# Masks of the attention scores written into PSUM by ScalarE and VectorE instead of by products with the identity

## The chip, the cores and the metric

The kernel runs on one core of one Trainium2 chip. The metric is the device time of one execution in microseconds. Engines are named as in the profile: PE is TensorE's matrix product, PEld its weight load, DVE is VectorE, ACT is ScalarE, POOL is GpSimd, SP is SyncE, which starts the transfers here.

## The reference, cut to what matters

One layer with two branches over x of shape 8 x 1024 x 256: after a layer norm, an attention branch and a branch of eight gated experts; their outputs and x are added. The experts' part is not touched. The attention:

```
xn = layernorm(x)
q, k, v = split(xn @ w_qkv + b_qkv), 16 heads of 16
scores = q @ k.T * 16 ** -0.5
4 global heads: scores masked where i - j < 0
12 local heads: scores masked where i - j < 0 or i - j > 64
ctx = softmax(scores) @ v
x = x + ctx @ w_out + b_out + experts(xn)
```

## The kernel before, in words

**Chunks.** The work goes in 16 chunks of 512 tokens (two for each of the 8 sequences; even chunks are the first half, odd ones the second). A planner (class `Plan` and the functions `add_...` and `..._groups`) writes down one list of stages, in one order, for all chunks. Every engine's program walks this one list and issues what is its own in each stage, so the order of each engine's queue is the order of the list. Semaphores join the engines. `weave(main, side)` mixes two lists of groups evenly.

**PSUM banks** are handed out by turns: each stage names the banks it uses (`uses`), and before a product writes into a bank, `take` waits until the reader of the bank's previous turn has counted up `bank_read[i]`.

**The attention is done in two passes.** The first finds for each query and head the maximum of the scores (*peaks*), the second computes the scores again with the maximum subtracted inside the product, as additional rows of the operands.
- *Local peaks*, stage `lpeak(t, grp)`, 12 a chunk: a product with the identity matrix lays the mask in a bank (L726, 512 columns), then eight products of 64 rows by 128 columns add the scores (L732). VectorE reduces the bank (L1197).
- *Global peaks*, stage `gpeak(t, j)`, 10 in an even chunk and 26 in an odd one: four products (L746), ahead of them a mask by the identity (L743) on the diagonal blocks only, 4 a chunk. VectorE reduces (L1204).
- Both use banks 5, 6 and 7 in turn. Counting them 0, 1, 2, ... over the two kinds, stage n can start when the reduction of stage n - 3 is done. Local peaks are stages 0 to 11. Diagonals are stages 12, 14, 17, 21 in an even chunk and 16, 22, 29, 37 in an odd one.
- *Local scores*, stage `lscore(grp, half, pair)`, 12 a chunk: mask by the identity (L766), eight products (L772), then ScalarE's exponential out of the bank (L1021). Banks 6 and 5 in turn, so score m can start when the exponential of m - 2 is done. The weighted sums of the values are L793, their transposes L837 (`cout`).
- *Global scores* follow (L807, L825) and are not masked by products.

**What is woven around them.** The peak stages of a chunk are woven, two at a time, into its experts (`x`, `c`: products of 512 columns, L587; `product`: the gates spread over a bank (L701), two VectorE products (L1273, L1276), ScalarE's PH copy (L1003); `mix`, L714; `open`, L675). ScalarE's copy `prod` out of `x` is L993. The stage `rows` turns the found maxima (L757), ScalarE copies them out of bank 4 (L1015) and a transfer brings them to the operands. The layer norm of the next chunk (`norm`, nine pieces on VectorE) is spread over the peak stages too. The local scores are woven with the next chunk's `turn` (transposes L605, ScalarE's XH copy L928, VectorE's subtraction XL L1145 and scan L1152) and `parts` (products L587, ScalarE L934, and three VectorE steps L1168, L1171, L1173). The order there, for one chunk (k is the score's number): scores 0, 1; turn 0; scores 2, 3; mix; values; turn 1; scores 4, 5; values; rows; scores 6, 7; parts(1,0); values, cout; parts(1,1); scores 8, 9; values; parts(0,0); scores 10, 11; parts(0,1); values, cout, values. The last chunk has no next one, and what is left of its experts is woven in instead.

Of the kernel before, what the change touches and what calls it, by code (L numbers as in the profile page):

```python
# [9 lines left out]
ACT = mybir.ActivationFunctionType  # L10
AX_X = mybir.AxisListType.X

P = 128
# [28 lines left out]
class Plan:  # L42
# [6 lines left out]
    def add(self, kind, *key, uses=()):  # L49
        self.stages.append((kind, *key))  # L50
        self.count[kind] = self.count.get(kind, 0) + 1
        self.place[(kind, *key)] = self.count[kind]
        for what in uses:
            self.turn[what] = self.turn.get(what, 0) + 1
            self.slot[(kind, *key), what] = self.turn[what]

# [9 lines left out]
def mixer_layer(  # L66
# [68 lines left out]

    def add_lpeak(ch, t, grp):
        add_on("lpeak", ch, t, grp, uses=[peak_use()])

    def add_gpeak(ch, t, j):
        add_on("gpeak", ch, t, j, uses=[peak_use()])  # L140

# [27 lines left out]

    def add_lscore(ch, grp, half, pair):  # L170
        add_on("lscore", ch, grp, half, pair, uses=[score_use(), exp_use()])

# [82 lines left out]
    def peak_groups(ch):  # L255
        c = ch % NC
        order = [[(add_lpeak, ch, t, grp)] for t in range(T) for grp in range(NL // 4)]
        order[-1].append((add, "found", ch, 0))
        gpeaks = [[(add_gpeak, ch, t, j)] for t in range(T) for j in range(c * T + t + 1)]
# [118 lines left out]
    with ctx:  # L378
# [136 lines left out]
        dve_step, pool_step, blank, cleared, selected, readied = (sem(n) for n in ("dve_step", "pool_step", "blank", "cleared", "selected", "readied"))  # L515
        global_masked = sem("global_masked")
        columns_ps, biases_in, split_hi, split_lo, turned_w, fold_ps = (sem(n) for n in ("columns_ps", "biases_in", "split_hi", "split_lo", "turned_w", "fold_ps"))
# [27 lines left out]
        def out_of_bank(*stage):  # L545

            i = bank_of(*stage)
            return bank_read[i], use(f"bank{i}", *stage)

        def on_diagonal(ch, j, half):  # L550
# [30 lines left out]
        def tensor_program(e):  # L581
# [12 lines left out]
            for stage in plan.stages:  # L594
# [124 lines left out]
                elif kind == "lpeak":  # L719
                    ch, t, grp = key  # L720
                    i, = where[stage]
                    which = 1 if ch % NC == 0 and t == 0 else 0
# [3 lines left out]
                    e.matmul(psum(i).rearrange("p (a k) -> p a k", a=4), ident_b[:, :],  # L726
                             peak_mask_l[:, which, :].unsqueeze(1).to_broadcast([P, 4, P]), start=True, stop=False, skip_group_check=True)
                    for a in range(4):
# [7 lines left out]
                elif kind == "gpeak":  # L736
# [3 lines left out]
                    q.wait_ge(global_in, 128 * (ch + 1))  # L740
                    take(i, *stage)
                    if diag:
                        e.matmul(psum(i).rearrange("p (a k) -> p a k", a=4), ident_b[:, :], peak_mask_g[:, :].unsqueeze(1).to_broadcast([P, 4, P]),  # L743
                                 start=True, stop=False, skip_group_check=True)
                    for g in range(NG):
# [14 lines left out]
                elif kind == "lscore":  # L760
# [3 lines left out]
                    q.wait_ge(ones_set, 2)  # L764
                    take(i, *stage)
                    e.matmul(psum(i).rearrange("p (w q) -> p w q", w=8), ident_b[:, :],  # L766
                             mask_l[:, :].unsqueeze(1).to_broadcast([P, 8, WINDOW]), start=True, stop=False, skip_group_check=True)
                    for a in range(2):
# [147 lines left out]
        def scalar_program(e):  # L916
            q = Seq(e)

            for stage in plan.stages:
# [75 lines left out]
                elif kind == "product":  # L995
# [7 lines left out]
                    e.activation(PH[:, h, :], prod[:, j % 3, :], ACT.Copy).then_inc(phi)  # L1003

                elif kind == "rows":
                    ch, which = key
# [90 lines left out]
        def vector_program(e):  # L1097
            q = Seq(e, dve_step)

            for stage in plan.stages:  # L1100
# [99 lines left out]
                elif kind == "gpeak":  # L1200
                    ch, t, j = key
                    i, = where[stage]
                    q.wait_ge(gpeaks_ps, nth(*stage))
                    e.tensor_reduce(block_peak[ch % NC][:, t, :, j], psum(i).rearrange("p (a k) -> p a k", a=4), AX_X, ALU.max).then_inc(bank_read[i])  # L1204

                elif kind == "found":
# [392 lines left out]
```

## Time and profile before

| | |
|---|---|
| median of 3 runs | 1655.23 us (1655.19 to 1657.1) |
| the profiled execution | 1654.62 us, span 1652.9 us |
| granted TensorE clock | 0.996 of full speed |
| TensorE busy (products) | 1563.5 us, 95% |
| VectorE busy | 937.7 us, 57% |
| ScalarE busy | 684.4 us, 41% |
| GpSimd busy | 284.2 us, 17% |

Busy times are unions of the instructions' spans on one engine. Consecutive products overlap in the trace, so the mean duration of one is longer than its place in the stream; the chain of waits gives the place.

### The profile page before, as it was taken

What the parts mean: (1) busy time and instruction counts of PE and PEld (TensorE: products, weight loads), DVE (VectorE), ACT (ScalarE), POOL (GpSimd) and SP (SyncE); (2) the same over time, 40 slices, a digit from 0 to 9 for tenths busy, and PEclk for the clock granted to TensorE, in tenths of its full rate; (3) what the DMA queues carried; (4) which work ended last, traced back from release to release, by engine and by line L of the source; (5) the groups of instructions that cost most, each with busy time, mean ns of one, the idle gap of its engine ahead of it and who ended that gap; (6) DMA issues with size and microseconds to landing.
All of it is one profiled execution on the core that took longest, in us unless ns stands there. A gap on an engine that the chain in (4) does not pass through costs nothing.

```text
span 1652.9 us, 36914 instructions
## 1 busy us (share of the span) xinstructions
PE 1563.5 (95%) x15489; PEld 1112.8 (67%) x15489; DVE 937.7 (57%) x2048; ACT 684.4 (41%) x1224; POOL 284.2 (17%) x346
## 2 busy tenths in 40 slices
PE   5899999999999999999999999999999999999997
PEld 4576675767757676676757767576675767667674
DVE  6665672737537484564837567274763748447461
ACT  3426245261543517243362523626254351634425
POOL 2011121211112111121201212021111201112111
PEclk9999999999999999999999999999999999999999
DMA  8514417072350906218071350806326080530800
GB/s 207 63 31 88 80 34 123 10 117 51 76 89 4 151 15 104 61 38 130 4 122 45 77 91 21 125 21 106 62 64 100 4 139 27 96 69 23 132 4 14
DMA packets 128186, 116.48 MB, mean 70 GB/s; under 512 B 19251, under 2 KB 127668, under 8 KB 127972
## 3 DMA queue, kind: packets, MB, share of 16 engines
q1 hardware_dynamic: 128020, 114.12, 38.5%
q8 instruction: 122, 2.00, 0.6%
q14 instruction: 44, 0.36, 0.1%
HBM read 73.43 MB, written 34.34 MB: 65 GB/s over the span
## 4 chain that ended last, share of the span: by engine, by line
PE 76%; DVE 14%; ACT 5%; issue 4%; POOL 1%; DMA 0%; DVEq 0%; ACTq 0%; POOLq 0%
PE PS L587 33%; PE PS L714 8%; DVE block_peak L1204 4%; PE PS L793 3%; PE PS L825 3%; PE PS L732 3%; PE PS L856 3%; PE PS L766 3%; PE PS L807 3%; PE PS L772 3%; DVE prod L1273 2%; PE PS L726 2%; DVE prod L1276 2%; ACT HE L1029 2%; PE PS L746 2%
## 5 line engine op out<-in xcount | busy, mean ns | idle before, releaser
L1446 POOL TENSOR_TENSOR PL<-prod,PH 128x512 fp32r<-128x512 f32 x128 | 164.5, 1285 | 792.7 <-ACT PH L1003 792.7
L1003 ACT ACTIVATE PH<-prod 128x512 fp32r<-128x512 f32 x128 | 80.8, 631 | 428.8 <-DVE prod L1276 428.8
L587 PE MATMUL PS<-XH,WH 128*128 128x512 f32 x512 | 220.4, 430 | 4.5 <-DVE XL L1145 1.9
L587 PE MATMUL PS<-XH,WL 128*128 128x512 f32 x512 | 203.6, 398 | 0.0
L587 PE MATMUL PS<-XL,WH 128*128 128x512 f32 x512 | 203.2, 397 | 0.0
L1204 DVE TENSOR_REDUCE block_peak<-PS 128x4 f32<-128x512 f32 x288 | 186.9, 684 | 4.2 <-PE PS L746 4.2
L993 ACT ACTIVATE prod<-PS 128x512 f32<-128x512 f32 x128 | 76.3, 596 | 231.3 <-PE PS L587 220.3
L1029 ACT ACTIVATE HE<-PS 128x512 f32<-128x512 f32 (+1 forms) x320 | 159.7, 552 | 26.1 <-PE PS L807 23.5
L1197 DVE TENSOR_REDUCE peak<-PS 128x4 f32<-128x512 f32 x192 | 125.6, 685 | 41.0 <-PE PS L732 41.0
L1273 DVE TENSOR_TENSOR prod<-PS,prod 128x512 f32<-128x512 f32 x128 | 88.1, 689 | 104.6 <-PE PS L701 104.6
L714 PE MATMUL PS<-UH,PH 128*128 128x256 f32 x512 | 139.5, 306 | 0.0
L1439 POOL TENSOR_SCALAR_AFFINE_SELECT HE<-HE 128x256 f32<-128x256 f32 x128 | 50.7, 409 | 478.9 <-ACT HE L1029 476.4
L1286 DVE RECIPROCAL cinv<-PS 128x16 f32<-128x16 f32 x64 | 16.3, 254 | 205.2 <-PE PS L837 205.2
L714 PE MATMUL PS<-UL,PH 128*128 128x256 f32 x512 | 126.0, 280 | 0.0
L587 PE MATMUL PS<-CH,WH 128*128 128x512 f32 x256 | 109.2, 427 | 9.1 <-DVE prod L1276 9.0
L587 PEld LDWEIGHTS PS<-XH,WH 128*128 128x128 f32 x512 | 96.9, 189 | 26.6 <-DVE WL L1341 2.2
L1021 ACT ACTIVATE HE<-PS 128x512 f32<-128x512 f32 x192 | 104.6, 596 | 21.5 <-PE PS L772 21.5
L587 PEld LDWEIGHTS PS<-XH,WL 128*128 128x128 f32 x512 | 96.7, 189 | 23.1
L807 PE MATMUL PS<-area 99*128 99x256 bf16 (+1 forms) x640 | 100.4, 267 | 7.8 <-ACT HE L1029 3.9
L587 PEld LDWEIGHTS PS<-XL,WH 128*128 128x128 f32 x512 | 97.3, 190 | 14.6
L746 PE MATMUL PS<-area 96*128 96x128 bf16 x1152 | 100.8, 220 | 5.8 <-DVE block_peak L1204 4.9
L807 PEld LDWEIGHTS PS<-area 99*128 99x128 bf16 x640 | 41.8, 98 | 93.5 <-ACT HE L1029 56.9
(195 smaller groups left out, 3154.8 us busy)
## 6 DMA issues: line engine op xcount, KB each, us to landing
parts_d<-area SPq DMA_DIRECT2D x32, 768.0 KB, 5.1
area<-parts_d SPq DMA_DIRECT2D x128, 192.0 KB, 12.4
area<-parts_d SPq DMA_DIRECT2D x32, 576.0 KB, 12.5
tok<-in_L_attn_x_dram SPq DMA_DIRECT2D x16, 512.0 KB, 6.5
xt<-in_L_attn_x_dram SPq DMA_DIRECT2D x16, 512.0 KB, 3.9
out_dram<-xt SPq DMA_DIRECT2D x16, 512.0 KB, 3.7
area<-parts_d SPq DMA_DIRECT2D x96, 64.0 KB, 5.9
Vs<-Va SPq DMA_DIRECT2D x24, 204.0 KB, 7.6
```

The source lines that it names most:

```text
L587: ins = e.matmul(ps, a, b, start=first and k == 0, stop=last and k == n - 1, skip_group_check=True)
L714: ins = e.matmul(out_half(t), (PH, PL)[part][:, h, t * P:(t + 1) * P], u[:, j, :], start=False, stop=False, skip_group_check=True)
L746: ins = e.matmul(psum(i, lo=P * g, hi=P * (g + 1)), QS[0:G16, g, t * P:(t + 1) * P], KG[0:G16, g, j * P:(j + 1) * P], start=(g == 0 and no ...
L807: ins = e.matmul(psum(i, lo=HALF * a + lo, hi=HALF * (a + 1)), KG[0:KSTK, g, j * P:(j + 1) * P], QS[0:KSTK, g, half * HALF + lo:(half + 1) ...
L993: e.activation(prod[:, j % 3, :], psum(2), ACT.Copy).then_inc(bank_read[2])
L1003: e.activation(PH[:, h, :], prod[:, j % 3, :], ACT.Copy).then_inc(phi)
L1021: e.activation(HE[:, k, :], psum(i), ACT.Exp, scale=SCALE).then_inc(bank_read[i])
L1029: e.activation(two(HE[:, k, :], lo), two(psum(i), lo), ACT.Exp, scale=SCALE).then_inc(bank_read[i])
L1197: e.tensor_reduce(peak[:, t, NG + 4 * grp:NG + 4 * (grp + 1)], psum(i).rearrange("p (a k) -> p a k", a=4), AX_X, ALU.max).then_inc(bank_re ...
L1204: e.tensor_reduce(block_peak[ch % NC][:, t, :, j], psum(i).rearrange("p (a k) -> p a k", a=4), AX_X, ALU.max).then_inc(bank_read[i])
L1273: e.tensor_tensor(prod[:, r, :], psum(4), prod[:, r, :], ALU.mult).then_inc(bank_read[4])
L1446: e.tensor_tensor(PL[:, j % 2, :], prod[:, j % 3, :], PH[:, j % 2, :].bitcast(F32), ALU.subtract).then_inc(plo)
```

## The change

The masks of most stages are no longer laid by a product. A new stage kind, `seed`, writes the mask into the bank ahead of the stage it belongs to: ScalarE does it for the peaks (an activation Copy of the broadcast bf16 mask into PSUM), VectorE for the local scores (a copy). The scores' products then add onto it. A seed stands in the list two stages ahead of its own stage: right behind peak n - 2 for peak n, right behind score m - 2 for score m. It waits until the bank's previous reader is done. Stages 0, 1 and 2 of the peaks and scores 0 and 1 of each chunk keep their identity product; peaks off the diagonal have no mask, as before. For this the banks of the peaks and scores are named when the groups are made, and the seed claims the bank in place of its stage (`claim`).

```diff
+    def add_scores(stage, uses):
+        bank, *slots = uses
+        laid = stage in where
+        if laid:
+            add(*stage, uses=slots)
+        else:
+            add(*stage, uses=uses)
+            where[stage] = [int(bank[-1])]
+        where[stage] += [int(u[-1]) for u in slots]
+
+    def add_seed(bank, *stage):
+        add("seed", *stage)
+        plan.claim(stage, [bank])
+        where[stage] = [int(bank[-1])]
...
     def local_groups(ch):
         units = [(grp, half) for grp in range(1, 1 + NL // 4) for half in range(2)]
+        scores = [(ch, grp, half, pair, score_use()) for grp, half in units for pair in range(2)]
         order = []
         for n, (grp, half) in enumerate(units):
-            order.append([(add_lscore, ch, grp, half, pair) for pair in range(2)])
+            order.append([])
+            for m in (2 * n, 2 * n + 1):
+                order[-1].append((add_lscore, *scores[m]))
+                if m + 2 < len(scores):
+                    order[-1].append((add_seed, scores[m + 2][4], "lscore", *scores[m + 2][:4]))
...
     def peak_groups(ch):
-        order = [[(add_lpeak, ch, t, grp)] for t in range(T) for grp in range(NL // 4)]
+        order = [[(add_lpeak, ch, t, grp, peak_use())] for t in range(T) for grp in range(NL // 4)]
+        gpeaks = [[(add_gpeak, ch, t, j, peak_use())] for t in range(T) for j in range(c * T + t + 1)]
+        for n, ((stage, *key),) in enumerate(order + gpeaks):
+            if stage is add_lpeak and n > 2:
+                order[n - 2].append((add_seed, key[-1], "lpeak", *key[:-1]))
+            elif stage is add_gpeak and key[2] == c * T + key[1]:
+                (order + gpeaks)[n - 2].append((add_seed, key[-1], "gpeak", *key[:-1]))
...
(TensorE, lpeak; lscore likewise with local_seeded, gpeak's diagonals likewise)
-                    take(i, *stage)
-                    e.matmul(psum(i)..., ident_b[:, :], peak_mask_l..., start=True, stop=False)
+                    if stage in laid:
+                        q.wait_ge(seeded, peaks_laid.index(stage) + 1)
+                    else:
+                        take(i, *stage)
+                        e.matmul(psum(i)..., ident_b[:, :], local_peak_mask(ch, t), start=True, stop=False)
...
(ScalarE)
+                elif kind == "seed":
+                    of, i = key, bank_of(*key)
+                    take = bank_read[i], use(f"bank{i}", *of) - 1
+                    if of[0] == "lpeak":
+                        q.wait_ge(*take)
+                        e.activation(psum(i)..., local_peak_mask(*of[1:3]), ACT.Copy).then_inc(seeded)
+                    elif of[0] == "gpeak":
+                        q.wait_ge(*take)
+                        e.activation(psum(i)..., peak_mask_g[:, :]..., ACT.Copy).then_inc(seeded)
...
(VectorE)
+                elif kind == "seed" and key[0] == "lscore":
+                    i = bank_of(*key)
+                    q.wait_ge(bank_read[i], use(f"bank{i}", *key) - 1)
+                    e.tensor_copy(psum(i)..., mask_l[:, :]...).then_inc(local_seeded)
```

## Rows read from the trace of the kernel before

**Rows 1.** The page: busy time by engine, and shares of the last chain.

```profile
PE 1563.5 (95%) x15489; PEld 1112.8 (67%) x15489; DVE 937.7 (57%) x2048; ACT 684.4 (41%) x1224; POOL 284.2 (17%) x346
...
PE 76%; DVE 14%; ACT 5%; issue 4%; POOL 1%; DMA 0%; DVEq 0%; ACTq 0%; POOLq 0%
```

**Rows 2.** Sums by stage: start:end length, then busy (instructions) of PE, PEld, DVE, ACT, POOL.

```profile
480.40:523.10 42.70, 41.32 (x325) 30.59 (x324) 32.03 (x71) 8.64 (x14) 9.64 (x8) 1.00 0.09 28
523.10:541.90 18.80, 18.80 (x354) 14.41 (x356) 11.82 (x21) 11.30 (x21) 4.44 (x5) 1.00 0.14 45
571.10:618.80 47.70, 46.04 (x388) 33.88 (x386) 39.90 (x85) 8.35 (x14) 9.00 (x7) 1.00 0.16 36
618.80:638.00 19.20, 19.02 (x357) 14.49 (x356) 12.81 (x25) 11.65 (x22) 5.06 (x5) 1.00 0.14 44
...
588.50:618.80 30.30, 29.29 (x229) 23.07 (x226) 27.57 (x66) 5.86 (x10) 5.75 (x5) 1.00 0.01 4
```

**Rows 3.** Groups by line, TensorE: count, busy us, mean ns, idle us before.

```profile
L726 PE MATMUL PS<-peak_mask_l,ident_b 128*128 128x512 bf16 x192 | 74.3, 387 | 0.6 <-DVE peak L1197 0.6
L766 PE MATMUL PS<-mask_l,ident_b 128*128 128x512 bf16 x192 | 74.1, 386 | 8.8 <-DVE block_peak L1204 8.8
```

**Rows 4.** The chain of waits, peaks 4 and 5 of chunk 5: start, us, what.

```profile
576.79 0.22 PE PS L726
...
577.35 0.32 PE PS L726
577.67 0.34 PE PS L732 x8
```

**Rows 5.** Groups by line, VectorE and ScalarE, each operation of 512 elements.

```profile
L1171 DVE CAST area<-rest 128x512 bf16<-128x512 f32 x64 | 27.4, 427 | 2.2
L1320 DVE MEMSET PS<- 128x512 f32 x2 | 1.0, 485 | 0.2
L1145 DVE TENSOR_TENSOR XL<-PS,XH 128x512 fp32r<-128x512 f32 x32 | 22.1, 692 | 33.7 <-ACT XH L928 33.6
L993 ACT ACTIVATE prod<-PS 128x512 f32<-128x512 f32 x128 | 76.3, 596 | 231.3 <-PE PS L587 220.3 <-POOL PL L1446 11.0
L1003 ACT ACTIVATE PH<-prod 128x512 fp32r<-128x512 f32 x128 | 80.8, 631 | 428.8 <-DVE prod L1276 428.8
```

**Rows 6.** ScalarE in order of time, peak stage of chunk 5: start, us.

```profile
576.57 0.63 ACT L1003 ACTIVATE PH<-prod 128x512 fp32r<-128x512 f32 x1 [2.84 <-DVE prod L1276]
...
601.47 0.63 ACT L1003 ACTIVATE PH<-prod 128x512 fp32r<-128x512 f32 x1 [2.56 <-DVE prod L1276]
```

**Rows 7.** TensorE in order of time, peak stage of chunk 5.

```profile
601.89 0.61 PE L746 MATMUL PS<-area 96*128 96x128 bf16 x8
```

**Rows 8.** The chain of waits, local stage of chunk 4.

```profile
525.53 1.50 PE PS L714 x12
...
529.09 0.57 PE PS L793 x32
...
529.87 0.32 PE PS L766
...
530.88 1.48 PE PS L587 x6
...
534.91 0.23 PE PS L766
...
538.92 1.48 PE PS L587 x6
```

**Rows 9.** VectorE in order of time, local stage of chunk 4.

```profile
524.24 0.18 DVE L1225 TENSOR_TENSOR peak_t_global<-peak_rest,peak_t_global 128x16 bf16<-128x16 f32 x1
...
529.46 1.27 DVE L1152 TENSOR_TENSOR_SCAN rest<-PS,carry,XH 128x512 f32<-128x512 f32 x1
...
536.92 0.69 DVE L1173 TENSOR_TENSOR area<-rest,area 128x512 bf16<-128x512 f32 x1
```

**Rows 10.** ScalarE in order of time, local stage of chunk 4.

```profile
523.74 1.08 ACT L1021 ACTIVATE HE<-PS 128x512 f32<-128x512 f32 x2 [1.33 <-PE PS L772]
```

More of the change, by code:

```diff
@@ L52, in add, with claim @@
         self.place[(kind, *key)] = self.count[kind]
+        self.claim((kind, *key), uses)
+    def claim(self, stage, uses):
         for what in uses:
             self.turn[what] = self.turn.get(what, 0) + 1
-            self.slot[(kind, *key), what] = self.turn[what]
+            self.slot[stage, what] = self.turn[what]
     def nth(self, kind, *key):
@@ L134, in mixer_layer, with add_lpeak, add_gpeak @@
     NORM = ("moments", "start", "square", "correct", "square", "correct", "square", "correct", "scale")
[L136 to L140, printed above, removed]
+    def add_lpeak(ch, t, grp, bank):
+        add_scores(("lpeak", ch, t, grp), [bank])
+    def add_gpeak(ch, t, j, bank):
+        add_scores(("gpeak", ch, t, j), [bank])
+    def add_scores(stage, uses):
[11 more added lines that the diff above has]
+        where[stage] = [int(bank[-1])]
     def add_turn(ch, k):
@@ L168, in add_mix, with add_lscore @@
         add("mix", ch, j, part, uses=[f"phl{j % 2}"] if part else [])
-    def add_lscore(ch, grp, half, pair):
-        add_on("lscore", ch, grp, half, pair, uses=[score_use(), exp_use()])
+    def add_lscore(ch, grp, half, pair, bank):
+        add_scores(("lscore", ch, grp, half, pair), [bank, exp_use()])
     def add_lav(ch, grp, half):
@@ L256, in peak_groups @@
         c = ch % NC
-        order = [[(add_lpeak, ch, t, grp)] for t in range(T) for grp in range(NL // 4)]
+        order = [[(add_lpeak, ch, t, grp, peak_use())] for t in range(T) for grp in range(NL // 4)]
[5 more added lines that the diff above has]
+                (order + gpeaks)[n - 2].append((add_seed, key[-1], "gpeak", *key[:-1]))
         order[-1].append((add, "found", ch, 0))
-        gpeaks = [[(add_gpeak, ch, t, j)] for t in range(T) for j in range(c * T + t + 1)]
         gpeaks[2].append((add_rows, ch, 0))
@@ L515, in mixer_layer @@
         dve_step, pool_step, blank, cleared, selected, readied = (sem(n) for n in ("dve_step", "pool_step", "blank", "cleared", "selected", "readied"))
-        global_masked = sem("global_masked")
+        global_masked, seeded, local_seeded = (sem(n) for n in ("global_masked", "seeded", "local_seeded"))
         columns_ps, biases_in, split_hi, split_lo, turned_w, fold_ps = (sem(n) for n in ("columns_ps", "biases_in", "split_hi", "split_lo", "turned_w", "fold_ps"))
@@ L548, in out_of_bank, with local_peak_mask @@
             return bank_read[i], use(f"bank{i}", *stage)
+        laid = [stage[1:] for stage in plan.stages if stage[0] == "seed"]
+        local_laid = [of for of in laid if of[0] == "lscore"]
+        peaks_laid = [of for of in laid if of[0] != "lscore"]
+        def local_peak_mask(ch, t):
+            return peak_mask_l[:, 1 if ch % NC == 0 and t == 0 else 0, :].unsqueeze(1).to_broadcast([P, 4, P])
         def on_diagonal(ch, j, half):
@@ L721, in tensor_program @@
                     i, = where[stage]
-                    which = 1 if ch % NC == 0 and t == 0 else 0
                     q.wait_ge(local_in, 128 * (ch + 1))
                     q.wait_ge(kept, ch + 1)
-                    take(i, *stage)
-                    e.matmul(psum(i).rearrange("p (a k) -> p a k", a=4), ident_b[:, :],
-                             peak_mask_l[:, which, :].unsqueeze(1).to_broadcast([P, 4, P]), start=True, stop=False, skip_group_check=True)
+                    if stage in laid:
+                        q.wait_ge(seeded, peaks_laid.index(stage) + 1)
+                    else:
+                        take(i, *stage)
+                        e.matmul(psum(i).rearrange("p (a k) -> p a k", a=4), ident_b[:, :], local_peak_mask(ch, t),
+                                 start=True, stop=False, skip_group_check=True)
                     for a in range(4):
@@ L740, in tensor_program @@
                     q.wait_ge(global_in, 128 * (ch + 1))
-                    take(i, *stage)
                     if diag:
-                        e.matmul(psum(i).rearrange("p (a k) -> p a k", a=4), ident_b[:, :], peak_mask_g[:, :].unsqueeze(1).to_broadcast([P, 4, P]),
-                                 start=True, stop=False, skip_group_check=True)
+                        q.wait_ge(seeded, peaks_laid.index(stage) + 1)
+                    else:
+                        take(i, *stage)
                     for g in range(NG):
@@ L764, in tensor_program @@
                     q.wait_ge(ones_set, 2)
-                    take(i, *stage)
-                    e.matmul(psum(i).rearrange("p (w q) -> p w q", w=8), ident_b[:, :],
-                             mask_l[:, :].unsqueeze(1).to_broadcast([P, 8, WINDOW]), start=True, stop=False, skip_group_check=True)
+                    if stage in laid:
+                        q.wait_ge(local_seeded, local_laid.index(stage) + 1)
+                    else:
+                        take(i, *stage)
+                        e.matmul(psum(i).rearrange("p (w q) -> p w q", w=8), ident_b[:, :],
+                                 mask_l[:, :].unsqueeze(1).to_broadcast([P, 8, WINDOW]), start=True, stop=False, skip_group_check=True)
                     for a in range(2):
@@ L1003, in scalar_program @@
                     e.activation(PH[:, h, :], prod[:, j % 3, :], ACT.Copy).then_inc(phi)
+                elif kind == "seed":
[3 more added lines that the diff above has]
+                        q.wait_ge(*take)
+                        e.activation(psum(i).rearrange("p (a k) -> p a k", a=4), local_peak_mask(*of[1:3]), ACT.Copy).then_inc(seeded)
+                    elif of[0] == "gpeak":
+                        q.wait_ge(*take)
+                        e.activation(psum(i).rearrange("p (a k) -> p a k", a=4), peak_mask_g[:, :].unsqueeze(1).to_broadcast([P, 4, P]),
+                                     ACT.Copy).then_inc(seeded)
                 elif kind == "rows":
@@ L1204, in vector_program @@
                     e.tensor_reduce(block_peak[ch % NC][:, t, :, j], psum(i).rearrange("p (a k) -> p a k", a=4), AX_X, ALU.max).then_inc(bank_read[i])
+                elif kind == "seed" and key[0] == "lscore":
+                    i = bank_of(*key)
+                    q.wait_ge(bank_read[i], use(f"bank{i}", *key) - 1)
+                    e.tensor_copy(psum(i).rearrange("p (w q) -> p w q", w=8),
+                                  mask_l[:, :].unsqueeze(1).to_broadcast([P, 8, WINDOW])).then_inc(local_seeded)
                 elif kind == "found":
```

## The prediction

> **What bounds the kernel now.** I read the page first, then the sums by stage, then the chain of waits, then single engines where the change lands. The page shows TensorE busy 95% of the span and on 76% of the chain that ended last [rows 1]: its instructions in order are the time, save where they wait. A pass over one chunk has three stages, and the windows show what stands beside TensorE in two of them [rows 2]. The peak stage of an even chunk takes 42.7 us with VectorE busy for 32.0; that of an odd chunk takes 47.7 with VectorE busy for 39.9, so the odd one is nearly bound by two engines. The local stage takes about 19 us with TensorE never idle (18.80 of 18.80) and VectorE busy for 11.8 to 12.8. The global stage isn't touched. So a TensorE instruction that goes is worth its place in the stream, if what replaces it is in time; the seeds that replace it sit in the fixed order of two other engines' queues, and that is where I look.
>
> **What goes.** Of the mask products, 144 of 192 on L726 (9 of 12 a chunk), 160 of 192 on L766 (10 of 12) and all 64 on L743 (4 a chunk, as the code has it) go [rows 3]. Their mean of about 386 ns is no price, since ends overlap. The chain gives the place they hold: 0.22 us for the first of a pair of peak products and 0.32 for the second, where the half-width products behind it start late; their eight products hold 0.34 [rows 4]. Per chunk that is 4 x 0.22 + 5 x 0.32 = 2.48 us for the local peaks (stage 3 is the second of its pair, then four pairs), 4 x 0.22 = 0.88 for the diagonals, and 10 x 0.22 = 2.2 for the local scores (0.32 once). Over 16 chunks: about 90 us, if nothing came late.
>
> **The price of a seed.** No row shows either operation: 512 bf16 read with a broadcast pattern, written to PSUM as f32. For ScalarE the nearest are 596 ns from PSUM and 631 from SBUF [rows 5]; I take 0.6 and see no reason for it to leave 0.55 to 0.65. For VectorE the bounds are far apart: the CAST of 512 elements within SBUF took 427 ns, a memset of 512 in PSUM 485, and the subtraction of 512 that reads PSUM 692 [rows 5]. I take 0.69: the only 512-element copy below it touches no PSUM, and the memset reads nothing.
> The Trainium skill speaks to this choice: "VectorE: DVE Perf Modes", section "Why PSUM operands drop a tier", says that the fast mode of a single-source operation with 32-bit data needs its tensors in SBUF and that with PSUM it runs at one element a cycle. By that rule 0.69 stands; by the CAST's row alone the sum below would come out at the price of the first rival. The trace has nothing that decides between them.
>
> **Peak stage, even chunks.** ScalarE has 8.6 us of work in 42.7 [rows 2], so 13 seeds x 0.6 = 7.8 us fit. A seed waits for the reduction three peaks earlier and for ScalarE's queue ahead of it. In most pairs 3 us or more of TensorE's other work lie between, and the seed is done in time. The exception is the pair of stages 4 and 5: their seeds are queued behind the PH copy of product 1. I put that wait at 0.3 us. VectorE has gaps enough in this stage, and its own work does not grow. Gain: 2.48 + 0.88 - 0.3 = 3.05, say 3.0 us a chunk, 24 us for eight.
>
> **Peak stage, odd chunks.** The pairs come closer. Pair 4, 5 follows pair 2, 3 with only four small products (L675) between. The PH copy of product 1 holds ScalarE from 576.57 to 577.20 [rows 6]; seed 4 follows to 577.8, seed 5 to 578.3, so that pair ends near 578.7 instead of 578.02 [rows 4]: +0.7 us, with stage 3's 0.32 already counted. The next three pairs have a transform or a mix ahead of each; they give 3 x 0.54 back, less 0.1, which makes -0.8 by the end of the local peaks. From there VectorE leads: 26 reductions of some 0.6 us, the normalization of the next chunk and the products leave it 2.7 us without work in the last 30.3 of the stage [rows 2], and what TensorE has gained is waited away. In this stretch two seeds are late. In stage 14's group the seed is queued ahead of ScalarE's `rows` copy, which frees bank 4 for product 3; that eats most of what is left, since product 3's VectorE step was due anyway. And stage 22's diagonal is seeded behind the PH copy of product 4, which ends at 602.10 [rows 6]: seeded at 602.7, while its products started at 601.89 before [rows 7]. That is +0.8, and product 5 follows it. Stage 29 repeats this with about 0.4, mostly absorbed by VectorE. I take +0.9 a chunk, seven chunks: 6.3 us lost. Bounds: -1.5 (to win: most of those 2.7 us, at no cost of waits) and +2. The last chunk is woven otherwise (no next chunk): -0.7.
>
> **Local stage.** Here VectorE gets 10 seeds, 6.9 us on top of 12, and they stand in its order among the next chunk's work. I follow the chain of chunk 4 [rows 8] with VectorE's rows [rows 9]; k is the number of the score stage, 0 to 11.
> - Seeds 2 and 3: VectorE is busy until 524.42 with the global peaks' parts [rows 9], and the exponentials of 0 and 1 end at 524.8 [rows 10]. Seeds end at 525.14 and 525.75; scores 3 end at 526.05 instead of 525.53. Two mask products are gone and the stage is still 0.5 late.
> - Seeds 4 and 5 follow VectorE's first turn (subtraction and scan); they end at 528.9, and scores 5 end at 529.18 instead of 529.09 [rows 8].
> - Seeds 6 and 7 are queued behind the second turn. Its scan ran from 529.46 to 530.73 [rows 9], and scores 6 began at 529.87 [rows 8], before the scan's end, which cost nothing. Now scores 6 must wait for it: the scan, 0.5 later with its turn, ends at 531.26, the seeds at 532.0 and 532.6, scores 7 at 532.9 instead of 530.88 [rows 8]: 2.0 late.
> - Scores 8 and 9 are free of this and win 0.45.
> - Seeds 10 and 11 are queued behind the three VectorE steps of parts(1,1). These ended 2.70 after the transform (534.91 to 537.61) [rows 8, 9]. The transform now ends at 536.94, so the steps at 539.64, the seeds at 540.37 and 540.98, scores 11 at 541.27 instead of 538.92 [rows 8].
> So the local stage becomes 2.35 us longer, 2.2 us of removed products included. With seeds at 0.43 the same walk ends at +1.0. Fifteen chunks: +35.2 us (15 at 0.43). The last chunk has no turns and parts in this stage and wins 1.3. Behind the stage nothing changes: VectorE has room there and the loads of the next stacks have tens of us until use.
>
> **The sum.** -24.0 + 6.3 - 0.7 + 35.2 - 1.3 = +15.5 us. The profiled execution took 1654.6 (span 1652.9), 0.6 below the median of 1655.2. 1654.6 + 15.5 = 1670.1, by the median 1670.7: 0.9% slower. What a measurement of this kernel can tell from no change is about 0.2%, 3.3 us, so the border runs at 1658.5.
>
> **Rivals.**
> 1. VectorE lays a mask in 0.43 us. The mechanism is the same, but each of the two exposed queues (turn 1, parts(1,1)) carries two seeds of 0.43: 1670.7 - 15 x 1.35 = 1650.5, faster. For it: the CAST's row. Against it: the VectorE row that has a source and a PSUM side took 692 [rows 5]. It decides from about 0.49 us a seed, where the local stage's loss (1.3) equals what the peak stages win. 13%.
> 2. The odd peak stages keep what their local peaks win (-1.0 instead of +0.9), because VectorE catches up in gaps that I count as closed: 1657.4, no change that could be told. For it: VectorE's 7.8 idle us in that stage. Against it: the order behind PH. 10%.
> 3. Nothing waits and the whole 90 us come off: 1565. For it: 95% TensorE. Against it: scores 6 began before the end of a scan that their seeds must follow. 4%.
> 4. The ScalarE seeds, waiting for reductions, hold up its transform copies and with them VectorE's products in every peak stage; the even chunks then win only 1.0 each: 1670.7 + 16 = 1687. For it: one queue for waits of two kinds. Against it: some 2 us of room before each copy in the even chunks. 12%.
> My forecast has the remaining 61%, with a range of its own of 1662 to 1680.
>
> **How the numbers follow.** Faster: rival 3, two thirds of rival 1, a little of rival 2: 0.15. Same: the rest of rival 1 and half of rival 2: 0.10. Slower: 0.75. The range from 1650 to 1684 leaves out rival 3, the far side of rival 1 and half of rival 4.
>
> **What the profile after will show.** Right: TensorE waits on L772 for VectorE's seed, in the third and the sixth pair of each local stage, 1.5 to 2 us and about 1; the local stage near 21.3 us, even peak stages near 39.7, odd ones near 48.5; a seed at 0.69 us on VectorE and 0.6 on ScalarE. In odd chunks the products of stages 4 and 22 wait for ScalarE. Wrong: a VectorE seed under 0.5 us, or local stages no longer than before.

## The result and the profile after

The changed kernel takes 1699.7 us (median of 4 runs, 1697.2 to 1702.4) against 1655.2 (4 runs, 1653.0 to 1657.1): the ratio is 1.0271, interval 1.0259 to 1.0283, so 2.7% slower. The forecast was 1670.7, and its range ended at 1684. The profiled execution took 1702.4 us with a span of 1700.7, 47.8 more than before, and its granted clock is 0.976 where it was 0.996.

The page of the changed kernel: busy time by engine, and the chain's shares, to be laid beside [rows 1].

```profile
PE 1515.6 (89%) x15121; PEld 1104.4 (65%) x15121; DVE 1033.3 (61%) x2208; ACT 805.4 (47%) x1432; POOL 282.7 (17%) x346
...
PE 66%; DVE 19%; ACT 8%; issue 5%; POOL 1%; DMA 0%; DVEq 0%; ACTq 0%; POOLq 0%
```

TensorE is busy for 48 us less in a span that is 48 us longer: it stands still for 96 us more. On the chain VectorE and ScalarE have gained 8 of the 10 points that TensorE lost. Who makes it stand still is in the sums by pair of the waits (the product that waits, the instruction that ends the wait, then total us, how often, the longest):

```profile
PE PS L817 <- DVE PS L1265: 60.2, 90, 2.1
PE PS L741 <- ACT peak_f L1071: 12.7, 7, 1.8
PE PS L774 <- ACT PS L1055: 12.6, 9, 1.6
PE PS L788 <- ACT PS L1058: 10.4, 14, 0.8
```

L817 is the local scores' product and L1265 VectorE's seed for it; L774 and L788 are the peaks' products, L1055 and L1058 ScalarE's seeds; L741 is `product`, L1071 ScalarE's `rows` copy. The seeds themselves, in the groups by line:

```profile
L1265 DVE CAST PS<-mask_l 128x512 f32<-128x512 bf16 x160 | 102.3, 684 | 14.1 <-ACT HE L1077 14.0
L1055 ACT ACTIVATE PS<-peak_mask_l 128x512 f32<-128x512 bf16 x144 | 82.7, 592 | 21.1 <-DVE peak L1253 21.0
L1058 ACT ACTIVATE PS<-peak_mask_g 128x512 f32<-128x512 bf16 x64 | 38.1, 595 | 31.3 <-DVE block_peak L1260 31.2
```

684 ns and 592 to 595: the prices taken were 0.69 and 0.6. Now the span, cut at the first mask product of each peak stage, at that of each local stage and at the last product of L838, and summed over the chunks of both traces:

| stages | before | after | difference | forecast |
|---|---|---|---|---|
| setup, to the first peak | 85.6 | 87.5 | +1.9 | 0 |
| 8 even peak stages | 342.5 | 314.5 | -28.0 | -24.0 |
| 7 odd peak stages | 334.2 | 346.4 | +12.3 | +6.3 |
| 15 local stages | 288.0 | 349.5 | +61.5 | +35.2 |
| 15 global stages | 507.0 | 507.6 | +0.7 | 0 |
| last chunk | 95.7 | 95.1 | -0.6 | -2.0 |

Together they make the 47.8 us; differences are taken before rounding. (The setup is of no account: its work isn't touched, and over all the kernels below its length lay anywhere between 84.2 and 87.5.) The local stages hold the loss and most of the miss. Their windows, first chunk 4's, then chunk 6's (columns as [rows 2], then granted clock, DMA share, GB/s):

```profile
534.32:555.80 21.48, 17.77 (x347) 13.66 (x347) 17.90 (x32) 11.85 (x21) 4.41 (x5) 1.00 0.12 40
737.16:760.15 22.99, 19.28 (x347) 14.65 (x347) 17.97 (x32) 11.85 (x21) 4.43 (x5) 0.93 0.11 37
```

Both hold the same 347 products, the same work on the other engines, and TensorE stands still for the same 3.71 us. Yet chunk 6 is 1.51 us longer, all of it in TensorE's busy time, and its granted clock is 0.93. Cut finer, four microseconds each at the same places of the two stages, chunk 4 first:

```profile
540.16:544.16 4.00, 1.87 (x64) 1.52 (x61) 3.06 (x4) 2.89 (x6) 2.00 (x3) 1.00 0.02 5
544.16:548.16 4.00, 4.00 (x52) 2.89 (x52) 2.90 (x5) 1.35 (x3) 0.41 (x1) 1.00 0.03 7
...
743.00:747.00 4.00, 1.87 (x64) 1.52 (x61) 3.06 (x4) 2.89 (x6) 2.00 (x3) 1.00 0.03 7
747.00:751.00 4.00, 4.00 (x45) 2.80 (x43) 1.83 (x3) 1.36 (x3) 0.41 (x1) 0.57 0.01 3
```

The first window of each holds the wait for score 6, with TensorE busy for 1.87 us of 4. They are alike to the last digit but for the transfers. Behind it chunk 4 goes on at full clock, while chunk 6 runs the next stretch at half of it, 1.2 GHz instead of 2.4, and gets 45 products done where chunk 4 got 52. Such a stretch at half clock is called a fall below; it counts for the stage in which it begins. The trace's record of the granted clock has 4 before, one in the setup and three in the last chunk, and 23 after: 13 of the 19 new ones in local stages and 6 in odd peak stages. In the odd peak stages the same pair can be set side by side, chunk 3 without and chunk 5 with a fall:

```profile
383.06:431.29 48.23, 42.50 (x375) 32.58 (x373) 40.01 (x85) 15.34 (x27) 8.93 (x7) 1.00 0.14 34
...
494.81:534.32 39.51, 37.75 (x312) 29.29 (x311) 31.94 (x71) 15.58 (x27) 9.60 (x8) 1.00 0.10 30
...
584.78:634.51 49.73, 43.99 (x375) 33.74 (x374) 40.02 (x85) 15.34 (x27) 8.94 (x7) 0.97 0.16 35
634.51:658.48 23.97, 19.41 (x349) 14.84 (x347) 19.07 (x36) 12.40 (x22) 5.03 (x5) 0.93 0.11 36
```

Idle 5.73 and 5.74, length 1.50 apart. So a fall costs 1.5 us, and 19 of them make 28.5 us. They were counted in the profiled execution: 1702.4 - 28.5 = 1673.9, 3.8 above the 1670.1 that was forecast for it. That they come so close is in part luck: without falls the stages miss by -4.0 (even peaks), -3.0 (odd peaks), +6.8 (local) and +4.0 (the rest), which nearly cancel. The second line is the even peak stage of chunk 4, 3.2 us shorter than in [rows 2]; the fourth is chunk 5's local stage, with a fall.

The waits themselves stand in order of time. TensorE in the local stage of chunk 4, products of the scores:

```profile
536.35 0.41 PE L817 MATMUL PS<-area 99*128 99x64 bf16 x8 [0.49 <-DVE PS L1265]
536.94 0.41 PE L817 MATMUL PS<-area 99*128 99x64 bf16 x8 [0.19 <-DVE PS L1265]
539.83 0.63 PE L817 MATMUL PS<-area 99*128 99x64 bf16 x16
543.19 0.41 PE L817 MATMUL PS<-area 99*128 99x64 bf16 x8 [1.95 <-DVE PS L1265]
543.77 0.41 PE L817 MATMUL PS<-area 99*128 99x64 bf16 x8 [0.18 <-DVE PS L1265]
548.07 0.64 PE L817 MATMUL PS<-area 99*128 99x64 bf16 x16
551.58 0.41 PE L817 MATMUL PS<-area 99*128 99x64 bf16 x8 [0.71 <-DVE PS L1265]
552.17 0.41 PE L817 MATMUL PS<-area 99*128 99x64 bf16 x8 [0.19 <-DVE PS L1265]
```

These are scores 2, 3, then 4 and 5 together, 6, 7, 8 and 9 together, 10, 11. VectorE in the same stretch:

```profile
535.59 1.29 DVE L1265 CAST PS<-mask_l 128x512 f32<-128x512 bf16 x2
...
541.26 1.27 DVE L1208 TENSOR_TENSOR_SCAN rest<-PS,carry,XH 128x512 f32<-128x512 f32 x1
542.46 1.26 DVE L1265 CAST PS<-mask_l 128x512 f32<-128x512 bf16 x2
...
550.23 0.69 DVE L1229 TENSOR_TENSOR area<-rest,area 128x512 bf16<-128x512 f32 x1
550.84 1.28 DVE L1265 CAST PS<-mask_l 128x512 f32<-128x512 bf16 x2
```

Seeds 6 and 7 start when the scan of the second turn is done, 10 and 11 behind the last step of parts(1,1): the two places that the forecast named. ScalarE in the peak stage of chunk 5:

```profile
590.27 0.63 ACT L1048 ACTIVATE PH<-prod 128x512 fp32r<-128x512 f32 x1 [2.28 <-DVE prod L1338]
590.81 1.62 ACT L1055 ACTIVATE PS<-peak_mask_l 128x512 f32<-128x512 bf16 x3
```

The PH copy waits for VectorE's product for 2.28 us, and the seeds of peak 4 and its followers wait behind it; peak 4 starts 1.40 us late.

### The profile page after: what moved, and what is told of

It reads as the page before. It is cut to its first block, busy times and chain, and to the rows that moved or that the text cites. A ratio compares the mean times of both kernels' runs of the same rounds, so it can differ in the third digit from the quotient of the medians.

```text
span 1700.7 us, 36626 instructions
## 1 busy us (share of the span) xinstructions
PE 1515.6 (89%) x15121; PEld 1104.4 (65%) x15121; DVE 1033.3 (61%) x2208; ACT 805.4 (47%) x1432; POOL 282.7 (17%) x346
## 3 DMA queue, kind: packets, MB, share of 16 engines
q8 instruction: 119, 1.95, 0.5%
## 4 chain that ended last, share of the span: by engine, by line
PE 66%; DVE 19%; ACT 8%; issue 5%; POOL 1%; DMA 0%; DVEq 0%; ACTq 0%; POOLq 0%
PE PS L627 33%; PE PS L754 8%; DVE PS L1265 3%; PE PS L788 3%; PE PS L870 3%; PE PS L901 3%; DVE prod L1335 3%; DVE prod L1338 3%; ACT HE L1085 2%; PE PS L852 2%; PE PS L838 2%; PE PS L882 2%; PE PS L774 2%; PE PS L956 2%; DVE block_peak L1260 2%
## 5 line engine op out<-in xcount | busy, mean ns | idle before, releaser
L627 PE MATMUL PS<-XH,WH 128*128 128x512 f32 x512 | 225.9, 441 | 4.4 <-DVE XL L1201 1.9
L627 PE MATMUL PS<-XH,WL 128*128 128x512 f32 x512 | 208.2, 407 | 0.0
L627 PE MATMUL PS<-XL,WH 128*128 128x512 f32 x512 | 207.8, 406 | 0.0
L754 PE MATMUL PS<-UH,PH 128*128 128x256 f32 x512 | 144.5, 314 | 0.0
L1077 ACT ACTIVATE HE<-PS 128x512 f32<-128x512 f32 x192 | 109.8, 597 | 52.9 <-PE PS L817 52.7
L754 PE MATMUL PS<-UL,PH 128*128 128x256 f32 x512 | 131.0, 288 | 0.0
L817 PE MATMUL PS<-area 99*128 99x64 bf16 x1536 | 73.9, 196 | 60.3 <-DVE PS L1265 60.2
L817 PEld LDWEIGHTS PS<-area 99*128 99x128 bf16 x1536 | 58.8, 99 | 87.5 <-DVE PS L1265 78.7
L1265 DVE CAST PS<-mask_l 128x512 f32<-128x512 bf16 x160 | 102.3, 684 | 14.1 <-ACT HE L1077 14.0
## 6 DMA issues: line engine op xcount, KB each, us to landing
area<-parts_d SPq DMA_DIRECT2D x32, 576.0 KB, 12.3
```

The lines of the kernel that those rows point to most:

```text
L627: ins = e.matmul(ps, a, b, start=first and k == 0, stop=last and k == n - 1, skip_group_check=True)
L754: ins = e.matmul(out_half(t), (PH, PL)[part][:, h, t * P:(t + 1) * P], u[:, j, :], start=False, stop=False, skip_group_check=True)
L817: ins = e.matmul(psum(i, lo=(4 * a + w) * WINDOW, hi=(4 * a + w + 1) * WINDOW), KL[0:KSTK, l, k0:k0 + P], QS[0:KSTK, NG + l, k0:k0 + WINDO ...
L1077: e.activation(HE[:, k, :], psum(i), ACT.Exp, scale=SCALE).then_inc(bank_read[i])
L1265: e.tensor_copy(psum(i).rearrange("p (w q) -> p w q", w=8), mask_l[:, :].unsqueeze(1).to_broadcast([P, 8, WINDOW])).then_inc(local_seeded)
```

## The experiments

All were timed beside the kernel before, which measured 1654.1 in the first set (e1 to e4), 1656.0 in the second (e5, e6, e7, e9) and 1654.9 with e10. The theory: the local scores' seeds come late in VectorE's queue, their waits cost what they are long, and the granted clock falls behind them and costs the rest. Rivals: the peaks' seeds cause it; the missing instructions or busier engines, not the waits, bring the clock down; VectorE has too much to do as such. One table for all, idle being TensorE's time without a product in the local stages of chunks 4 and 5 and in the peak stage of chunk 5. Idle and falls are those of the one profiled execution, which needn't be the median one:

| kernel | median, ratio (interval) | idle, us | falls in local, odd peak stages |
|---|---|---|---|
| before | 1655.2 | 0.0, 0.2, 1.7 | 0, 0 |
| changed | 1699.7, 1.0271 (1.0259 to 1.0283) | 3.7, 4.6, 5.7 | 13, 6 |
| e1 | 1638.9, 0.992 (0.9895 to 0.9946) | 0.0, 0.4, 5.7 | 0, 10 |
| e2 | 1711.5, 1.0344 (1.0327 to 1.0361) | 3.7, 4.3, 1.6 | 9, 0 |
| e3 | 1684.8, 1.0184 (1.0168 to 1.0199) | 0.8, 1.8, 5.6 | 0, 9 |
| e4 | 1609.5, 0.9729 (0.9714 to 0.9743) | 0.0, 0.2, 2.5 | 0, 0 |
| e5 | 1668.4, 1.0069 (1.0045 to 1.0094) | 2.0, 2.9, 5.7 | 2, 10 |
| e6 | 1632.4, 0.9862 (0.9847 to 0.9876) | 0.0, 0.4, 5.0 | 0, 5 |
| e7 | 1633.6, 0.9869 (0.9854 to 0.9884) | 0.0, 0.4, 5.4 | 0, 2 |
| e9 | 1617.8, 0.9783 (0.9765 to 0.9802) | 1.4, 1.6, 2.4 | 0, 0 |
| e10 | 1600.0, 0.9666 (0.965 to 0.9682) | 0.1, 0.3, 2.4 | 0, 0 |

**e1, the peaks' seeds alone.**

```diff
-                if m + 2 < len(scores):
+                if m + 2 < len(scores) and False:
```

> The changed kernel with the masks of all local scores laid by TensorE again; the 13 ScalarE seeds a chunk for the peaks stay. Theory (queue waits, and a granted clock that falls after them): local stages back to 18.8 us at clock 1.000; even peak stages 3.5 us shorter than before, as in the changed kernel's trace (39.2 for 42.7), so 8 x -3.5 = -28; odd peak stages between +0.5 (clock 1.000, as in chunk 3 of the changed kernel) and +1.9 a chunk: 1655 - 28 + 3 to 14 = 1630 to 1641, faster than before. Rival (writing PSUM from other engines slows TensorE's own products everywhere): slower than 1655. Rival (the loss sits in the odd peak stages alone): near 1690.

The median is 15 us below that of the kernel before. The local stage of chunk 4 and the peak stage of chunk 5:

```profile
517.12:536.14 19.02, 19.02 (x357) 14.54 (x357) 12.02 (x22) 11.29 (x21) 4.45 (x5) 1.00 0.14 46
...
565.11:616.24 51.13, 45.41 (x376) 35.44 (x374) 40.16 (x85) 15.35 (x27) 8.94 (x7) 0.93 0.16 34
```

The local stage is back at 19.0, and the 15 together take 289.6 us: all but 1.5 of their 61.5 us come from the scores' seeds. The peak stage stands still for 5.7 us as in the changed kernel, but here the clock fell twice in it; over the seven odd ones it fell ten times. The five executions differ by as much: 1636.8 us at a mean clock of 0.992, 1648.4 at 0.984. The trace is of the last of these, the slowest, so ten falls are more than the median execution had.

**e2, the scores' seeds alone.**

```diff
-            if stage is add_lpeak and n > 2:
+            if stage is add_lpeak and False:
...
-            elif stage is add_gpeak and key[2] == c * T + key[1]:
+            elif stage is add_gpeak and key[2] == c * T + key[1] and False:
```

> The changed kernel with all masks of the peaks laid by TensorE again; only VectorE's 10 seeds a chunk for local scores 2 to 11 stay. Theory: peak stages as before (42.7 and 47.7), local stages 22.5 (even) and 23.7 (odd) where the clock falls, 21.0 and 22.2 where it does not: 1655 + 15 x 2.8 + 0 to 15 falls x 1.5 us = 1697 to 1720. If the waits of odd peak stages were needed for the fall of the clock in local stages, the low end. Rival (the peaks' seeds carry the loss): under 1665.

57 us slower; less e1's 15 that makes 42 of the 44.5. Peak stages are as before. Local stages without and with a fall (chunks 7 and 4):

```profile
841.77:864.25 22.48, 17.96 (x349) 13.73 (x347) 18.84 (x36) 12.21 (x22) 5.03 (x5) 1.00 0.11 38
...
536.48:559.45 22.97, 19.26 (x347) 14.71 (x347) 17.96 (x32) 11.87 (x21) 4.43 (x5) 0.93 0.11 37
```

**e3, zero products in the waits.** Nothing is left out; ahead of the waits of scores 2, 6 and 10 TensorE adds products with a tile of zeros onto a bank, 13 a chunk.

```diff
+                        for _ in range({2: 2, 6: 8, 10: 3}.get(4 * (grp - 1) + 2 * half + pair, 0) if ch + 1 < CHUNKS else 0):
+                            e.matmul(psum(0)..., ident_b[:, :], zeros_b[:, :]..., start=False, stop=False)
```

> The changed kernel with products of zeros added onto bank 0 ahead of the waits of local scores 2 (two), 6 (eight) and 10 (three), 512 columns each, in all chunks but the last: TensorE does more, but stands still for less; the seeds come as late as before. Theory (half of the local stages' loss is the granted clock, which falls to 1.2 GHz because TensorE stood still): local stages at clock 1.000, 21.0 even and 22.2 odd, 13 falls x 1.5 us gone: about 1680 against 1700. Rival (the clock falls for another reason, and waits alone are the loss): 1700 or, with 2.8 us of products a chunk that don't fit, up to 1715.

This separates the length of a wait from the fall behind it. The local stages of chunks 4 and 5:

```profile
528.98:550.47 21.49, 20.71 (x360) 14.76 (x360) 17.91 (x32) 11.87 (x21) 4.43 (x5) 1.00 0.12 40
...
628.95:651.64 22.69, 20.88 (x362) 14.82 (x360) 19.05 (x36) 12.42 (x22) 5.02 (x5) 1.00 0.11 38
```

Chunk 4's stage is as long as in the changed kernel (21.49, 21.48), with 13 more products in it. The local falls are gone, 13 to 0, and the local stages together went from 349.5 to 330.7 us. The whole is 14.9 us faster though TensorE does more. VectorE is as busy as before, so its load doesn't bring the clock down; TensorE standing still does. (The zero products also make up for the missing mask products; that these don't matter is seen in e5 and e10.) The odd peak stages, not filled, went on falling.

**e4, only the seeds that come in time.** The peaks' seeds without stages 4 and 5 and without diagonals in odd chunks, of the scores' seeds only 8 and 9, none in the last chunk.

```diff
-                if m + 2 < len(scores):
+                if m + 2 < len(scores) and m + 2 in (8, 9) and nxt_(ch):
...
-            if stage is add_lpeak and n > 2:
+            if stage is add_lpeak and n > 2 and nxt_(ch) and (c == 0 or n not in (4, 5)):
...
-            elif stage is add_gpeak and key[2] == c * T + key[1]:
+            elif stage is add_gpeak and key[2] == c * T + key[1] and c == 0:
```

> Only those seeds that the walk through the queues finds in time: all 13 in even chunks' peak stages, in odd ones local peaks 3 and 6 to 11 (not 4 and 5, no diagonals), local scores 8 and 9 (of 10), nothing in the last chunk; the rest is laid by TensorE. Theory: even peak stages -3.5 x 8 = -28, odd ones -1.0 x 7 = -7 (VectorE nearly bound there), local stages -0.45 x 15 = -6.7, clock 1.000 outside the last chunk: 1613. If odd stages give nothing, 1620. Rival (each seed costs something of its own beside the wait it causes): over 1635.

2.7% faster than the kernel before. Chunk 4's peak and local stage, then chunk 5's:

```profile
469.02:508.28 39.26, 37.55 (x312) 29.26 (x310) 31.87 (x71) 15.58 (x27) 9.61 (x8) 1.00 0.10 30
508.28:526.87 18.59, 18.59 (x355) 14.34 (x355) 13.31 (x24) 11.31 (x21) 4.46 (x5) 1.00 0.14 45
555.85:602.16 46.31, 43.86 (x382) 33.17 (x380) 39.81 (x85) 12.47 (x21) 9.01 (x7) 1.00 0.16 37
602.16:621.12 18.96, 18.77 (x357) 14.40 (x355) 14.26 (x28) 11.64 (x22) 5.05 (x5) 1.00 0.14 45
```

With fewer seeds than the changed kernel it is 90 us faster. The seeds left win 3.5 us in each even peak stage, 0.45 in each local one and 1.4 in each odd peak stage, where the places of their products come to 1.9 (0.32 + 3 x 0.54) and TensorE waits 0.8 us more than before.

**e5, the second turn behind scores 4 and 5.** One stage moves in the list; every seed stays.

```diff
+        scores_on = local_groups(ch)
+        if nxt:
+            scores_on[3].append((add_turn, ch + 1, 1))
```

> The changed kernel with one stage moved: the next chunk's second turn stands behind local scores 4 and 5 instead of ahead of them, so VectorE's seeds 6 and 7 come ahead of its subtraction and scan. Theory (seeds 6 and 7 were late because they were queued behind the scan): the wait ahead of scores 6 falls from 1.95 to 2.09 us to nearly 0, scores 7 waits about 0.35, parts(1,0) about 0.4 for the turn; local stages 19.6 (even) and 20.6 (odd) and fewer falls of the clock: about 1660 against 1700. Rival (a VectorE seed is late by itself, wherever it stands, through the exponential and two handovers): the wait stays above 1 us, 1690 or more.

31 us less than the changed kernel, from the place of one stage in the list; with it VectorE's subtraction and scan stand behind seeds 6 and 7. The local stage of chunk 4:

```profile
523.55:543.39 19.84, 17.89 (x347) 13.64 (x347) 17.81 (x32) 11.85 (x21) 4.45 (x5) 1.00 0.13 43
```

Score 6 waits no more; scores 2 (0.49 in even, 0.98 in odd chunks) and 10 (0.70) still do. VectorE is as busy as in the changed kernel (17.81 and 17.90), so its load isn't the cause. TensorE has the same 347 products as there, and the local falls went from 13 to 2: the missing products aren't the cause either.

**e6, the PH copy behind the seeds,** on e1: ScalarE holds it back until the seeds of the peaks that follow are issued.

```diff
+                if held and kind not in ("lpeak", "gpeak", "seed", "norm", "found"):
+                    lay_ph(*held.pop())
...
-                    e.activation(PH[:, h, :], prod[:, j % 3, :], ACT.Copy).then_inc(phi)
+                    held.append(key)
```

> The kernel with the peaks' seeds alone, and ScalarE's PH copy of each product moved in its queue behind the seeds of the peaks that follow the product. Theory (in odd chunks seeds 4, 22 and 29 are late because PH stands ahead of them): the waits ahead of peaks 4 (1.40), 22 (0.82) and 29 (0.66) go to about 0, 0 and 0.3, but seed 5 still waits for reduction 2 behind product 1 on VectorE, so peak 5 waits about 1.2; odd peak stages near 47 us with fewer falls of the clock, against 48.2 to 51.0: 1618 to 1628 against 1639. Rival (the seeds wait for VectorE's reductions, not for PH): no change, 1635 to 1642.

6.5 us less than e1 by the medians, 0.6% by the ratios, and less than was expected. The wait of peak 4 went from 1.40 to 0, but peak 5 then waited 1.14, as had been expected: its seed starts at 568.16 us, when the VectorE reduction that frees its bank ends, and that one stands behind product 1's two VectorE steps (566.12 and 566.84). Peak 29, expected at about 0.3, still waits 0.67 for the same reason, behind the steps of product 5. The odd stage of chunk 5, with one fall in it: 48.96, which is 47.5 without.

```profile
562.07:611.03 48.96, 44.01 (x375) 34.11 (x374) 40.72 (x85) 15.05 (x27) 9.00 (x7) 0.97 0.16 36
```

**e7, the `rows` stage ahead of the seed in the third global peak's group,** on e1.

```diff
-        gpeaks[2].append((add_rows, ch, 0))
+        gpeaks[2].insert(1, (add_rows, ch, 0))
```

> The kernel with the peaks' seeds alone, and in odd chunks ScalarE's copy of the turned maxima (stage rows) ahead of the seed of peak 16 instead of behind it. TensorE's wait for that copy ahead of product 3 (1.8 us each) goes. Theory of the prediction (VectorE leads there and that wait is absorbed): 0 to 0.5 us a chunk, 1635 to 1639, perhaps one or two falls of the clock less. Rival (the wait counts in full, and it takes the clock with it): 1.8 us and up to 1.4 of clock a chunk, 1618 to 1626.

`product` 3's wait of 1.8 went, but peak 16 now waits 1.06 for its seed and peak 19 0.43. The stages of chunk 5 (no fall) and chunk 7 (one):

```profile
562.86:610.78 47.92, 42.54 (x376) 32.60 (x374) 39.95 (x85) 15.43 (x27) 8.95 (x7) 1.00 0.17 37
757.03:806.31 49.28, 43.96 (x375) 33.87 (x374) 40.03 (x85) 15.43 (x27) 8.97 (x7) 0.97 0.15 34
```

A stage without a fall is 0.3 us shorter than the changed kernel's, 2 us over seven. The median lies 5.3 below e1's (0.5% by the ratios), and the trace has two falls where e1's has ten, but that is mostly e1's own spread: at the same mean clock of 0.992 e1 took 1636.8 and 1637.3 us and e7 1634.1 and 1634.8, some 2.6 us less and so near the 2 us. So of the 1.8 us waited for `rows` nearly all came back as other waits, and whether the shift spares falls isn't shown.

**e9, ScalarE lays the masks of scores 4 to 11,** on e4.

```diff
-                if m + 2 < len(scores) and m + 2 in (8, 9) and nxt_(ch):
+                if m + 2 < len(scores) and m + 2 > 3 and nxt_(ch):
...
+                        e.activation(psum(i)..., mask_l..., ACT.Copy).then_inc(local_seeded)
```

> The kernel with the seeds in time, but local scores 4 to 11 are seeded by ScalarE, which also reads the bank two stages before (VectorE seeds nothing; scores 2 and 3 keep TensorE's mask). Theory (where a seed stands decides, and right behind the exponential that frees the bank it is early): nothing waits, 8 x 0.22 less than before in each local stage, against 0.45 with two seeds: 1609.5 - 15 x 1.3 = 1590. Rival (ScalarE, 11.3 us busy in 18.8 before, gets 4.8 more, and its copies for turns and parts come late): local stages no shorter than 18.2 (even), 1605 to 1620.

Its own rival came true: scores 6 and 7 wait 0.57 and 0.74, their seeds standing behind ScalarE's copies and exponentials. The local stage of chunk 4, ScalarE busy for 15.9 of 19.2:

```profile
510.27:529.44 19.17, 17.72 (x349) 13.88 (x349) 11.68 (x21) 15.93 (x29) 4.46 (x5) 1.00 0.09 31
```

**e10, e4's peaks, ScalarE's seeds for scores 4, 5 and 8 to 11, and e6's PH copy.** Scores 2, 3, 6 and 7 keep the product.

```diff
+                if m + 2 < len(scores) and m + 2 in (4, 5, 8, 9, 10, 11) and nxt_(ch):
```

> The kernel with the seeds in time, with ScalarE's seeds for local scores 4, 5, 8, 9, 10 and 11 (2, 3, 6 and 7 keep TensorE's mask; 6 and 7 waited 0.57 and 0.74 us when ScalarE seeded all of 4 to 11) and PH behind the seeds. Theory: local stages 18.6 - 6 x 0.22 = 17.3 (even) and 17.7 (odd), no waits for seeds in them; even peak stages 38.8 instead of 39.2: 1609.5 - 15 x 0.85 - 8 x 0.4 = 1593.5, clock 1.000 outside the last chunk. Rival (ScalarE's own work comes late wherever it gets six more copies in the stage, and something else waits, as the cost of 1.3 us a stage that all eight showed beyond their own 1.3 us of waits): 1605 or more.

1600.0 us, 3.3% faster than the kernel before and 5.9% than the changed one. Chunk 4's peak and local stage, and chunk 5's:

```profile
464.85:503.75 38.90, 37.31 (x312) 29.26 (x310) 31.94 (x71) 15.54 (x27) 9.60 (x8) 1.00 0.10 30
503.75:521.83 18.08, 17.93 (x351) 14.05 (x351) 11.67 (x21) 14.64 (x27) 4.44 (x5) 1.00 0.12 38
550.83:597.15 46.32, 43.88 (x381) 33.18 (x380) 39.82 (x85) 12.41 (x21) 8.97 (x7) 1.00 0.19 39
597.15:615.60 18.45, 18.13 (x353) 14.11 (x351) 12.61 (x25) 14.97 (x28) 5.05 (x5) 1.00 0.11 37
```

It is 6.5 us above what was expected: against e4 the local stage gives 0.5 us where 0.85 had been counted.

## Why the prediction was right in kind and wrong in size

**The step that failed** is the sum "-24.0 + 6.3 - 0.7 + 35.2 - 1.3 = +15.5 us": it prices each wait by its own length. Its term "Fifteen chunks: +35.2 us" measured +61.5, and "6.3 us lost" in the odd peak stages measured +12.3. The granted clock has no term in the sum; it was put at nothing without a word. What stands in their place: TensorE standing still is followed in many stages by a stretch at 1.2 GHz, which costs 1.5 us: 13 in local and 6 in odd peak stages, 28.5 us together. e3 showed it by filling the waits without shortening them. The page before had a granted clock of 0.996 and three late falls, in the last chunk, where the work is thin; I had read it as a constant.
The Trainium skill has the rule that was wanted: "TensorE: Matmul & The Clock Gate", section "A second HAM failure mode: psum-queue depth-cycling", tells of a kernel whose TensorE idles briefly between groups of products as it goes through the PSUM banks, often enough for its clock to fall and rise again and again. The trace agrees: no wait for a seed was over 2.1 us, and 19 falls were added.

Without the falls, the local stages would be 61.5 - 19.5 = +42.0, and the odd peak stages 12.3 - 9.0 = +3.3. Point by point:

- **Price of a seed.** 0.69 and 0.6 forecast, 0.684 and 0.592 to 0.595 measured. Rival 1 (0.43 on VectorE) is dead. The 684 ns also fit the rule of the Trainium skill's "VectorE: DVE Perf Modes" that was weighed against the CAST's row; that PSUM, and not the bf16 source or the broadcast pattern, sets them was not tried by itself.
- **Local stage, even chunks.** +2.35 forecast, +2.44 measured without a fall (21.48 against 19.04 by the same cuts). The stage starts 11.23 us later than in the trace of [rows 8]; moved by that, the forecast had scores 6 start at 543.23 and the last seed end at 552.21; the trace has 543.19, and score 11 starting at 552.17. Here the walk along two queues was exact to 0.05 us.
- **Local stage, odd chunks.** They were taken to be like the even ones. They lose 3.1 (chunk 5's 23.97, less a fall of 1.5, against 19.38 before) to 3.3 (e3's 22.69). In chunk 5 score 2 waits 0.98 instead of 0.50 and score 6 2.09 instead of 1.95, which is 0.6 of it. Of the 6.8 between 42.0 and 35.2 the even chunks make 0.7; the odd ones, 0.75 to 0.95 over the forecast seven times, 5.3 to 6.6. The stage had been walked in chunk 4 only.
- **Even peak stages.** -3.0 forecast, -3.5 measured: peaks 4 and 5 have 0.00 and 0.10 of wait where 0.3 was put, so all of what the products' places gave came off. Rival 4, which wanted them to win 1.0, is dead.
- **Odd peak stages.** +0.9 forecast, +0.46 measured without a fall (48.2 against 47.7). The places were right: peak 4 waits 1.40, peak 22 0.82, peak 29 0.66, and `product` 3 1.8 for the `rows` copy. TensorE stands still 4.1 us more a stage for 3.5 less of work (46.04 busy in [rows 2], 42.50 now). Rival 2, which had them win, didn't come, and rival 3, in which nothing waits, is far off.
- **Last chunk.** -2.0 forecast, -0.6 measured: its peaks 3 and 6 wait 1.21 and 1.62 for their seeds, a place that was not walked.
- **Signs.** The waits came where the walk had them, 1.95 ahead of scores 6 and 0.71 ahead of scores 10 (plus 0.50 ahead of scores 2). The sign called these the third and the sixth pair; scores 6 and 7 are the fourth. Local stages of even chunks are 21.5 without a fall, even peak stages 39.3 to 39.5. Only the odd ones, forecast at 48.5, came at 48.2 or at 49.7, and that spread was the sign of the clock.

**What stays open.** What decides whether the clock falls in a given stage: chunks 4 and 6 of the changed kernel do the same with the same waits, and only one falls. In the table idle time and falls go together, but not in step: e2's local stages stand still for 61 us in all, the changed kernel's for 62, and fell 9 times, not 13; in e1 the peak stages of chunks 1 and 5 both stand still for 5.7 us, and the first had no fall (48.2 us), the second two (51.1). Nor was it found why the clock of one kernel differs between executions, 0.984 to 0.992 for e1.

## What to carry to other kernels

A product taken off the bound engine is worth its place in the stream only if what replaces it is ready in the other engine's order: look at what stands ahead of it in that queue, instruction by instruction, and keep the product where a scan, or a copy that itself waits, stands there; e4 did so and turned +2.7% into -2.7%. Price a new stall of TensorE at its length and then again for the clock: here 19 stretches at half clock came with the new stalls and cost 1.5 us each, 28.5 in all, nearly twice the forecast's whole 15.5. And where stages come in two kinds, walk each kind: the odd chunks' local stages lost a third more than the even ones' (3.2 and 2.4 us, falls taken off).

## What the runs showed of the hardware that was not expected

- The same local stage with the same waits (3.71 us) ran once at a clock of 1.00 and took 21.48 us, and once at 0.93 and took 22.99, in one execution; the stretch after the wait did 52 products in one case and 45 in the other.
- Products with zeros in the waits held the clock: local falls 13 to 0 with 13 of them a chunk, and chunk 4's stage no longer for them (21.49 and 21.48 us).
- ScalarE writes 512 bf16 from SBUF as f32 into PSUM in 592 to 595 ns, less than the 631 that a copy of 512 f32 takes within SBUF [rows 5] and as much as the 596 out of PSUM. VectorE takes 684 ns for it, where its CAST within SBUF takes 427 [rows 5] and its subtraction that reads PSUM 692.
